# Fetching the last 128 rows of every group with SyncE and ScalarE row by row, in a three-layer graph network on one core

## The chip, the cores and the metric

One Trainium2 chip, one of its cores. The metric is the device time of one execution in microseconds (us). The kernel before was run three times.

## The reference

A layer norm of 6250 nodes of 256 features goes through three layers of a relational graph network with 200,000 edges of 8 types, and a feed-forward step whose log-sum form is a product of magnitudes and a product of signs.

```python
N, E, D, R, L = (6250, 31250, 256, 8, 3)      # 200000 edges are passed in
for l in range(n_layers):
    xr = jnp.einsum('nd,rde->rne', x, W_rel[l])
    msg = xr[edge_type, src]
    agg = jax.ops.segment_sum(msg, dst, num_segments=x.shape[0])
    x = jax.nn.relu(agg + x @ W_root[l] + bias[l])
...
x = x + _L0_gnn_ref(_layernorm(x, axis=-1), edge_index, edge_type_8, W_rel, W_root, bias)
x = x + _L0_ffn_ref(_layernorm(x, axis=-1)[None], weight, ffn_bias)[0]
```

In `_L0_ffn_ref`, out = sign(sign(x) @ sign(w).T) * (|x| @ |w|.T) + bias, scaled by the largest magnitudes of rows.

## The kernel before, in words

The edges are sorted by destination. A **triple** is 3 chunks of 128 edges, a **group** is 9 triples; there are 58 groups, and 49 tiles of 128 nodes. The node features of a layer lie in HBM (`node_table`, two of them, read and written in turn). Each layer goes through the 58 groups in order. In a group:

- GpSimd (`POOL`, L433) gathers the source rows of each chunk with one indirect DMA: 128 rows of 1 KB into `rows`, which holds one group's 27 chunks. The gather for a triple waits until TensorE has multiplied the triple nine before (`seg_ready`), and signals `gathered[k]`.
- TensorE (L454, `products`) multiplies the rows of triple k by a one-hot matrix, 12 matmuls of 128x128 in fp32. VectorE adds the result to `agg` (L1057, `agg_added`), and makes the next group's one-hots (L966).
- Behind the second triple of the next group TensorE multiplies `agg` by the relation weights, 32 matmuls (L523, `transform`). VectorE adds the result to the node sums `acc` (L1079, L1080), and ScalarE clears that half of `agg` (L755); the halves are used in turn by even and odd groups.
- Where a group is the first of a tile's, the tile before it has ended, and the group carries that tile's last steps (below: a *late* group). In layers 0 and 1 ScalarE makes `new_x` (L813) and stores it (L816), TensorE turns it behind triple 4, ScalarE copies it (`nextT`, L770), TensorE multiplies it behind triple 7, ScalarE copies the sum into `acc` (L762). In the last layer VectorE makes the layer norm and the magnitudes in the gaps behind triples 0 to 2; ScalarE gives the square root (L774), the sign (`sgn`, L784), the copies of what TensorE turned (`magT`, `sgnT`, L790, L791), the sign of the product (`osgn`, L797) and the output's store (L804). Each of these waits for another engine's step.
- In layer 0 SyncE also loads an `x_tile` per group, which TensorE turns behind triple 4 of its group, and ScalarE copies it to `xT` (L745).

In every **odd** group the last chunk isn't gathered by GpSimd: SyncE reads 128 byte offsets (`far_at`, L287, a load of 32 registers at a time) and issues 128 DMAs of one row each into `far_rows` (L354), once the even group before the last one fetched is multiplied (`multiplied`, L359). So GpSimd issues 27 gathers in an even group, 26 in an odd one, and 24 in the last group, whose last triple is empty.

```python
def fetch(layer, i, q):
    for p, start in zip(range(q * LOADS, (q + 1) * LOADS), far_starts(i, q)):
        sp.dma_start(far_row(p), far_from(layer, start)).then_inc(far_by_sp[layer][p // HALF], 16)
```

The order of each engine's work is written out by hand, and each engine issues its own in order. GpSimd's is unrolled; SyncE, ScalarE and TensorE have loops: SyncE one of 24 and one of 4 turns in layer 0 and one of 28 turns in each later layer, two groups a turn. A new layer's gathers start when the layer before has stored its last tile.

## Time and profile before

| | |
|---|---|
| median of 3 runs | 5928.23 us (5927.94 to 5928.28) |
| the profiled execution | 5926.47 us, its span 5924.7 us |
| GpSimd busy | 4371.6 us, 74% |
| TensorE busy (matmuls) | 4305.1 us, 73% |
| VectorE busy | 1828.7 us, 31% |
| ScalarE busy | 619.3 us, 10% |
| granted TensorE clock, mean | 0.894 |

The span runs from the first to the last instruction of the profiled execution. Busy time leaves out what issues DMAs, and register, branch and semaphore instructions, so SyncE has no busy time, and its work is read from its DMA queue's rows (`SPq`; `ACTq` is ScalarE's). An engine that is busy for 74% can still set the pace, if it can't issue faster.

### The profile page before, as it was taken

Reading aid. Unit: us, or ns where it says so; the run is one execution under the profiler, and the core shown is the slowest. Engines: PE = TensorE matmul, PEld = TensorE weight load, DVE = VectorE, ACT = ScalarE, POOL = GpSimd, SP = SyncE. Lnnn points to the kernel's source line nnn. Section 1 sums busy time; section 2 is a strip of 40 time slices with the busy share of each in tenths; the row PEclk is TensorE's granted clock in tenths of the full one; section 3 lists DMA queues with packets and bytes.
Section 4 is the critical chain, followed back from the end, with each engine's and each line's share of the span. In section 5 each row is a group of like instructions: output and inputs, shape, how many; then the busy total and the mean of one; then the engine's idle time right before and its main releaser. Section 6 shows DMA issues by size and latency. Waiting matters only on the chain.

```text
span 5924.7 us, 107591 instructions
## 1 busy us (share of the span) xinstructions
PE 4305.1 (73%) x26040; PEld 3885.7 (66%) x26041; DVE 1828.7 (31%) x3534; ACT 619.3 (10%) x848; POOL 4371.6 (74%) x4631
## 2 busy tenths in 40 slices
PE   3777777787787677777777777767777777677776
PEld 3666666676676666666666666656766667666666
DVE  4222222222222222222222222223334334333333
ACT  3101010101010000010001000001111011101111
POOL 5777777777777677777777777767777777777775
PEclk7989999989989899998999999989888888888898
DMA  6433343433443333333333333333333333333332
GB/s 196 116 113 115 114 115 114 115 114 114 114 116 114 104 111 111 110 111 110 110 110 111 110 110 111 110 104 112 113 113 115 113 113 114 113 112 114 112 113 85
DMA packets 301812, 672.72 MB, mean 114 GB/s; under 512 B 89440, under 2 KB 154181, under 8 KB 301670
## 3 DMA queue, kind: packets, MB, share of 16 engines
q0 software_dynamic: 221040, 603.88, 35.6%
q1 hardware_dynamic: 51928, 41.07, 2.3%
q10 hardware_dynamic: 28702, 26.46, 1.3%
q14 instruction: 124, 1.02, 0.1%
q8 instruction: 18, 0.29, 0.0%
HBM read 645.38 MB, written 25.68 MB: 113 GB/s over the span
## 4 chain that ended last, share of the span: by engine, by line
POOL 38%; PE 29%; issue 18%; DMA 8%; DVEq 2%; ACT 2%; DVE 2%; ACTq 0%; SPq 0%; POOLq 0%
POOL rows L433 38%; PE bank L454 16%; PE bank L523 11%; DMA rows<-node_table,idx 7%; ACT agg L755 2%; DVE agg L1057 1%; PE bank L655 1%; DVEq L1040 1%; DVEq L1043 1%; DVEq L1147 1%; PE bank L581 0%; PE bank L662 0%; PE bank L653 0%; ACT x_in L708 0%; DVE onehot L966 0%
## 5 line engine op out<-in xcount | busy, mean ns | idle before, releaser
L433 POOL DMA_INDIRECT rows<-node_table,idx x4605 | 4364.3, 948 | 1504.1 <-issue 1300.8
L454 PE MATMUL bank<-onehot,rows 128*128 128x128 f32 x18444 | 2683.6, 305 | 1431.6 <-DMA rows<-node_table,idx 665.1
L454 PEld LDWEIGHTS bank<-onehot,rows 128*128 128x128 f32 x18444 | 2520.7, 217 | 1597.7 <-issue 1578.5
L1057 DVE TENSOR_TENSOR agg<-bank,agg 128x256 f32 x1566 | 664.2, 424 | 2168.9 <-PE bank L454 1652.0
L523 PE MATMUL bank<-wrel,agg 128*128 128x256 f32 x5568 | 1266.3, 387 | 15.3 <-issue 14.0
L523 PEld LDWEIGHTS bank<-wrel,agg 128*128 128x128 f32 x5568 | 1071.3, 195 | 164.4 <-issue 21.6
L966 DVE TENSOR_TENSOR onehot<-bank,key 128x1152 f32<-128x1152 f32 x525 | 707.3, 1347 | 0.2
L755 ACT COPY agg<-zero_col 128x2304 f32 x174 | 367.3, 2111 | 2973.8 <-PE bank L523 2973.8
L1079 DVE SCALAR_TENSOR_TENSOR acc<-bank,in_first,acc 128x256 f32 x174 | 84.1, 484 | 1806.9 <-PE bank L523 1682.3
L762 ACT COPY acc<-bank 128x256 f32 (+1 forms) x98 | 36.5, 372 | 1071.4 <-PE bank L655 1071.4
L655 PE MATMUL bank<-wroot,nextT 128*128 128x256 f32 x392 | 146.3, 509 | 0.0
L655 PEld LDWEIGHTS bank<-wroot,nextT 128*128 128x128 f32 x392 | 85.0, 240 | 54.9 <-issue 45.1
L643 PE MATMUL bank<-ident_bf,sgn 128*128 128x128 bf16 x98 | 14.1, 228 | 108.2 <-issue 101.8
L653 PE MATMUL bank<-bias_bc,one_row 1*128 1x256 f32 x196 | 89.8, 547 | 1.5 <-ACT nextT L770 1.5
L643 PEld LDWEIGHTS bank<-ident_bf,sgn 128*128 128x128 bf16 x98 | 6.3, 97 | 117.4 <-issue 117.4
L1080 DVE SCALAR_TENSOR_TENSOR acc<-bank,in_second,acc 128x256 f32 x174 | 82.6, 475 | 0.0
L581 PE MATMUL bank<-wroot,xT 128*128 128x256 f32 x232 | 76.6, 464 | 0.0
L770 ACT COPY nextT<-bank 128x256 f32<-128x256 f32 x98 | 36.5, 372 | 374.9 <-PE bank L636 374.9
L1070 DVE TENSOR_TENSOR agg<-agg 128x256 f32<-128x256 f32 (+1 forms) x174 | 73.1, 420 | 0.0
L454 PE MATMUL bank<-onehot,far_rows 128*128 128x128 f32 x348 | 72.3, 292 | 0.0
L581 PEld LDWEIGHTS bank<-wroot,xT 128*128 128x128 f32 x232 | 55.5, 243 | 10.4
L454 PEld LDWEIGHTS bank<-onehot,far_rows 128*128 128x128 f32 x348 | 57.9, 209 | 0.0
(140 smaller groups left out, 844.7 us busy)
## 6 DMA issues: line engine op xcount, KB each, us to landing
far_rows<-node_table SPq DMA_DIRECT2D x10752, 1.0 KB
rows<-node_table,idx POOLq DMA_INDIRECT x4605
node_table<-new_x ACTq DMA_DIRECT2D x98, 128.0 KB
x_tile<-node_table SPq DMA_DIRECT2D x58, 128.0 KB
x_in<-in_x_dram SPq DMA_DIRECT2D x8, 768.0 KB, 11.2
wrel<-in_L_gnn_W_rel_dram SPq DMA_DIRECT2D x6, 1024.0 KB, 6.9
xres<-in_x_dram ACTq DMA_DIRECT2D x48, 128.0 KB
out_dram<-res ACTq DMA_DIRECT2D x48, 128.0 KB
```

Source lines behind the costliest of these rows:

```text
L433: pool.indirect_dma_start(rows[:, s:s + D], None, tables[layer % 2], bass.IndirectOffsetOnAxis(ap=idx[:, g * TPG + k, j:j + 1], axis=0),). ...
L454: last = nc.tensor.matmul(to[:, h, :], row, hot[:, hot_k * CH + j, :], start=(j == 0), stop=(j == CH - 1))
L523: last = nc.tensor.matmul(out_ps, agg[:, half * KH + h, r, 0:P], wrel[:, h, r * D:(r + 1) * D], start=(r == 0 and h == 0), stop=(r == R - ...
L581: last = nc.tensor.matmul(root_ps, xT[:, h, :], wroot[:, 0, h, :], start=(h == 0), stop=(h == KH - 1))
L653: nc.tensor.matmul(next_ps, one_row[:, :], bias_bc[0:1, layer + 1, :], start=True, stop=False)
L655: last = nc.tensor.matmul(next_ps, nextT[:, h, :], wroot[:, layer + 1, h, :], start=False, stop=(h == KH - 1))
L755: nc.scalar.copy(agg[:, ds(g % 2 * KH, KH), :, :].rearrange("p h r s -> p (h r s)"), zero_col[:, :].to_broadcast([P, KH * R * SLOTS])).the ...
L966: return nc.vector.tensor_tensor(onehot[:, b, :, :], place_ps.unsqueeze(1).to_broadcast([P, BATCH * CH, P]), key[:, ds(g * TPG + b * BATCH ...
L1057: nc.vector.tensor_tensor(window, seg[k % 3].rearrange("p h (r w) -> p h r w", r=R), window, ALU.add).then_inc(agg_added, 1)
L1070: nc.vector.tensor_tensor(agg[:, half, :, 0:WIN], agg[:, half, :, 0:WIN], agg[:, half, :, P:SLOTS], ALU.add).then_inc(agg_ready, 1)
L1079: nc.vector.scalar_tensor_tensor(sums_of(first), out_ps, in_first[:, ds(g, 1)], sums_of(first), ALU.mult, ALU.add)
L1080: nc.vector.scalar_tensor_tensor(sums_of(first + 1), out_ps, in_second[:, ds(g, 1)], sums_of(first + 1), ALU.mult, ALU.add).then_inc(group ...
```

## The change

- All groups but the last (57 of 58) have their last 128 rows fetched row by row: `far_rows` has two halves, for even and odd groups. GpSimd issues 26 gathers in each of them: 4518 in all instead of 4605.
- SyncE fetches 74 of the 128 rows of each group, ScalarE's queue 54. Both read the same `far_at`.
- SyncE fetches a group when the group two before it has been multiplied. Its loops are unrolled by four groups: 14 turns each, 12 and 2 in layer 0.
- ScalarE fetches the rows of the group behind its own while it works on a group. In layers 0 and 1 it issues 22 rows (`fetch_third`), then copies `next_ps` into `acc`, then 32 rows (`fetch_fourth`). In the last layer's late groups it issues 10 rows ahead of `magT`, 12 ahead of `osgn`, 10 ahead of the output's store and 22 behind it. Each batch stands twice in the program, once for each half of `far_rows`, with a branch.
- At the start of a layer both fetch group 0, ScalarE ahead of its first group.
- TensorE waits ahead of triple 8 for the two gathered chunks, two semaphores of SyncE and one of ScalarE.

```diff
-FETCHED = GROUPS // 2 - 1
-HALF = P // 2
+FETCHED = GROUPS - 1
 LOADS = 32
 QUARTERS = P // LOADS
+SP_ROWS = 74
+ACT_ROWS = P - SP_ROWS
+SP_HALF = SP_ROWS // 2
+ACT_TURNED, ACT_SIGNED = 20, 10
+SP_UNROLL = 4
...
+        far_rows = sb("far_rows", [P, 2 * D], fp32)
...
+            def multiplied(layer, g):
+                if not isinstance(g, int):
+                    sp.wait_ge(agg_added, g * TPG + (layer * TRIPLES + 3 - TPG))
+                    sp.sem_inc(sp_mark, 1)
+            def fetch(layer, g, b, q):
+                first, end = q * LOADS, min(SP_ROWS, (q + 1) * LOADS)
+                for p, start in zip(range(first, end), far_starts(SP, g, q, 0, end - first)):
+                    sp.dma_start(far_row(p, b), far_from(layer, start)).then_inc(far_by_sp[layer][b][p // SP_HALF], 16)
+            def first_layer(g, b, tile):
+                multiplied(0, g)
+                fetch(0, g, b, 0)
+                fetch(0, g, b, 1)
+                load_tile(g, tile)
+                fetch(0, g, b, 2)
             load_tile(0, 0)
             sp.wait_ge(far_at_ready, 1)
-            def first_layer(i, odd, even):
-                multiplied(0, i)
-                for q in range(QUARTERS // 2):
-                    fetch(0, i, q)
-                load_tile(i * 2 + 1, odd)
-                for q in range(QUARTERS // 2, QUARTERS):
-                    fetch(0, i, q)
-                load_tile(i * 2 + 2, even)
-            with sp.Fori(0, (TILES - 1) // 2) as i:
-                first_layer(i, i * 2 + 1, i * 2 + 2)
-            with sp.Fori((TILES - 1) // 2, FETCHED) as i:
-                first_layer(i, TILES - 1, TILES - 1)
+            for q in range(QUARTERS - 1):
+                fetch(0, 0, 0, q)
+            with sp.Fori(0, (TILES - 1) // SP_UNROLL) as i:
+                for m in range(1, SP_UNROLL + 1):
+                    first_layer(i * SP_UNROLL + m, m % 2, i * SP_UNROLL + m)
+            with sp.Fori((TILES - 1) // SP_UNROLL, FETCHED // SP_UNROLL) as i:
+                for m in range(1, SP_UNROLL + 1):
+                    first_layer(i * SP_UNROLL + m, m % 2, TILES - 1)
             load_tile(GROUPS - 1, TILES - 1)
             for layer in range(1, L):
                 sp.wait_ge(out_ready, layer * GROUPS)
                 load_weights(layer)
                 sp.wait_ge(stored, 16 * TILES * layer + 16)
-                with sp.Fori(0, FETCHED) as i:
-                    multiplied(layer, i)
-                    for q in range(QUARTERS):
-                        fetch(layer, i, q)
+                for q in range(QUARTERS - 1):
+                    fetch(layer, 0, 0, q)
+                with sp.Fori(0, FETCHED // SP_UNROLL) as i:
+                    for m in range(1, SP_UNROLL + 1):
+                        g = i * SP_UNROLL + m
+                        multiplied(layer, g)
+                        for q in range(QUARTERS - 1):
...
-                        for j in range(CH - 1 if g % 2 and k == TPG - 1 else CH):
+                        for j in range(CH - 1 if k == TPG - 1 else CH):
...
+            def far_landed(layer, g, b):
+                pe.wait_ge(gathered[TPG - 1], g * (16 * (CH - 1)) + (layer * FETCHED + 1) * (16 * (CH - 1)))
+                for h in range(2):
+                    pe.wait_ge(far_by_sp[layer][b][h], g * (8 * SP_HALF) + (2 - b) * 8 * SP_HALF)
+                pe.wait_ge(far_by_act[layer][b], g * (8 * ACT_ROWS) + (2 - b) * 8 * ACT_ROWS)
...
+            act.wait_ge(far_at_ready, 1)
+            def fetch_part(layer, g, b, q, first, end=LOADS):
+                for m, start in enumerate(far_starts(SCALAR, g, q, first, end)):
+                    act.dma_start(far_row(q * LOADS + first + m, b), far_from(layer, start)).then_inc(far_by_act[layer][b], 16)
+            def multiplied(layer, g):
+                if not isinstance(g, int):
+                    act.wait_ge(agg_added, g * TPG + (layer * TRIPLES + 3 - TPG))
+                    act.sem_inc(act_mark, 1)
+            def fetch_third(layer, g, b):
+                multiplied(layer, g)
+                fetch_part(layer, g, b, QUARTERS - 2, SP_ROWS % LOADS)
+            def fetch_fourth(layer, g, b):
+                fetch_part(layer, g, b, QUARTERS - 1, 0)
+            def fetch_by_turn(layer, g, b):
+                multiplied(layer, g)
+                fetch_part(layer, g, b, QUARTERS - 2, SP_ROWS % LOADS, ACT_TURNED)
+            def fetch_by_product(layer, g, b):
+                fetch_part(layer, g, b, QUARTERS - 2, ACT_TURNED)
+            def fetch_by_sign(layer, g, b):
+                fetch_part(layer, g, b, QUARTERS - 1, 0, ACT_SIGNED)
+            def fetch_by_store(layer, g, b):
+                fetch_part(layer, g, b, QUARTERS - 1, ACT_SIGNED)
+            def fetch_ahead(layer, g, part):
+                with act.If(g < FETCHED - 1):
+                    ahead = nc.s_assert_within(g + 1, 1, FETCHED - 1, skip_runtime_bounds_check_because="the branch is taken in front of the last fetched group")
+                    with act.If(g % 2 > 0):
+                        part(layer, ahead, 0)
+                    with act.Else():
+                        part(layer, ahead, 1)
+                    act.sem_inc(act_mark, 1)
             def group(layer, g, late=None):
                 gg = g + layer * GROUPS
                 if late:
@@ -743,13 +799,28 @@
                     act.wait_ge(xT_ps_ready, gg + 2)
                     act.sem_inc(act_mark, 1)
                     nc.scalar.copy(xT[:, :, :], xT_ps).then_inc(xT_ready, 1)
-                if late:
+                if layer < L - 1:
+                    fetch_ahead(layer, g, fetch_third)
+                    if late:
+                        with act.If(g < late[0]):
+                            next_sums(layer, late[1])
+                    fetch_ahead(layer, g, fetch_fourth)
+                elif late:
                     with act.If(g < late[0]):
-                        if layer < L - 1:
-                            next_sums(layer, late[1])
-                        else:
-                            turned_tile(late[1])
-                            out_of_tile(late[1])
+                        fetch_ahead(layer, g, fetch_by_turn)
+                        turned_tile(late[1])
+                        fetch_ahead(layer, g, fetch_by_product)
+                        sign_of_tile(late[1])
+                        fetch_ahead(layer, g, fetch_by_sign)
+                        out_of_tile(late[1])
+                        fetch_ahead(layer, g, fetch_by_store)
+                    with act.Else():
+                        fetch_ahead(layer, g, fetch_third)
+                        fetch_ahead(layer, g, fetch_fourth)
+                        act.sem_inc(act_mark, 1)
+                else:
+                    fetch_ahead(layer, g, fetch_third)
+                    fetch_ahead(layer, g, fetch_fourth)
                 act.wait_ge(out_ready, gg + 1)
                 act.sem_inc(act_mark, 1)
                 nc.scalar.copy(agg[:, ds(g % 2 * KH, KH), :, :].rearrange("p h r s -> p (h r s)"),
@@ -790,11 +861,14 @@
                 nc.scalar.copy(magT[:, :, :], mag_ps).then_inc(magT_ready, 1)
                 nc.scalar.copy(sgnT[:, :, :], sgn_ps).then_inc(sgnT_ready, 1)
-            def out_of_tile(t, last=False):
...
+                if layer:
+                    act.wait_ge(stored, 16 * TILES * layer + 16)
+                fetch_third(layer, 0, 0)
+                fetch_fourth(layer, 0, 0)
```

SyncE's first loop in layer 0, first of the kernel before: the loads of 32 offsets, the rows, and `x_tile` in the middle (L348, L350). These are the rows behind the loop's head at L372.

```order
L372 ISA
L287 ISA
L287 TENSOR_LOAD far_at
L354 DMA far_rows<-node_table 1x1024 x32
L287 ISA
L287 TENSOR_LOAD far_at
L354 DMA far_rows<-node_table 1x1024 x32
L348 ISA
L350 ISA
L350 DMA x_tile<-node_table 128x256
```

The same place now. The piece from the loop's head to the batch of 10 is one group, and it stands four times in the loop.

```order
L379 ISA
L292 ISA
L292 TENSOR_LOAD far_at
L366 DMA far_rows<-node_table 1x1024 x32
L292 ISA
L292 TENSOR_LOAD far_at
L366 DMA far_rows<-node_table 1x1024 x32
L353 REGISTER_ALU
L355 ISA
L355 DMA x_tile<-node_table 128x256
L292 ISA
L292 TENSOR_LOAD far_at
```

What moved: a turn of the loop was two groups with 128 rows and two `x_tile`; it is now four groups with 296 rows and four `x_tile`.

ScalarE in the last layer, inside the loop over tiles, from the copy of the turned magnitudes to the output's store. Before:

```order
L790 COPY magT<-bank 128x256
L791 COPY sgnT<-bank 128x256
L797 ACTIVATE osgn<-bank 128x256
L798 REGISTER_ALU
L804 ISA
L804 DMA out_dram<-res 128x256
```

Now, from `osgn` on (the batch of 12 rows stands ahead of it in the same form):

```order
L868 ACTIVATE osgn<-bank 128x256
L785 COMPARE_AND_BRANCH
L787 REGISTER_ALU
L787 COMPARE_AND_BRANCH
L292 ISA
L292 TENSOR_LOAD far_at
L756 DMA far_rows<-node_table 1x1024 x10
L787 UNCONDITIONAL_BRANCH
```

What moved: between two steps that stood next to each other there are now two branches, a register load and ten row DMAs; the second branch chooses between two copies of the batch. The loop over tiles has 216 row DMAs in the program, of which a group issues 54; the loops of the first two layers have 108.

## Rows read from the trace of the kernel before

**Rows 1.** GpSimd's gathers by their line: ns min/median/max, first and last start in us

```profile
L433 POOL DMA_INDIRECT rows<-node_table,idx x4605: 942/946/1241, 50.9 to 5882.9; - x192
```

**Rows 2.** Timeline, GpSimd, early, and where the last layer starts

```profile
92.27 0.95 POOL L433 DMA_INDIRECT rows<-node_table,idx  x1 [7.27 <-PE bank L454]
...
3956.96 0.94 POOL L433 DMA_INDIRECT rows<-node_table,idx  x1 [29.91 <-DMA node_table<-new_x]
3958.21 0.95 POOL L433 DMA_INDIRECT rows<-node_table,idx  x1 [0.30 <-issue]
```

**Rows 3.** Waits of TensorE, second layer, 2015 to 3965: us, times, longest

```profile
PE bank L454 <- DMA rows<-node_table,idx: 321.3, 207, 3.3
```

**Rows 4.** Waits of TensorE, last layer, 3965 to 5884

```profile
PE bank L454 <- DMA rows<-node_table,idx: 92.4, 61, 2.7
```

**Rows 5.** Timeline, ScalarE's clears of agg around three late groups

```profile
4674.05 2.11 ACT L755 COPY agg<-zero_col 128x2304 f32 x1 [30.06 <-PE bank L523]
...
4773.21 2.11 ACT L755 COPY agg<-zero_col 128x2304 f32 x1 [12.92 <-PE bank L523]
```

**Rows 6.** Waits of TensorE in those three groups, 4674.0 to 4773.2

```profile
PE bank L454 <- DVE agg L1057: 18.5, 6, 4.7
```

**Rows 7.** The chain that ended last, 4674 to 4708

```profile
by line: PE bank L454 42.2%; PE bank L523 21.1%; issue 16.4%; DVEq L1147 2.9%; DVE agg L1057 2.6%; PE bank L662 2.5%; DVEq L1040 2.5%; DVEq L1043 2.4%; PE bank L645 1.2%; DVEq L1057 0.8%; PE bank L643 0.8%; DVEq L1150 0.8%; PE bank L664 0.6
```

**Rows 8.** Waits of TensorE in the group before, 4641.9 to 4674.0

```profile
PE bank L454 <- DMA rows<-node_table,idx: 5.2, 3, 2.2
```

**Rows 9.** By source line: row DMAs, load of 32 registers, load of 2

```profile
L354 SPq DMA_DIRECT2D far_rows<-node_table x10752: 224/225/314, 87.0 to 5810.6; - x200
...
L287 SPq TENSOR_LOAD <-far_at x336: 2024/2036/2457, 84.8 to 5798.4; - x168
...
L827 ACTq TENSOR_LOAD <-end_row x144: 485/725/976, 154.7 to 5872.7; - x144
```

**Rows 10.** SyncE's queue in its first loop: timeline, and its wait

```profile
1024.16 22.99 SPq L354 DMA_DIRECT2D far_rows<-node_table  x64
1047.49 0.36 SPq L350 DMA_DIRECT2D x_tile<-node_table  x1
1060.73 0.27 SPq L354 DMA_DIRECT2D far_rows<-node_table  x1
...
SPq L359 <- DVE agg L1057: 10.1, 1, 10.1
```

**Rows 11.** The same place in its second loop

```profile
1711.81 0.37 SPq L350 DMA_DIRECT2D x_tile<-node_table  x1
1724.22 0.98 SPq L354 DMA_DIRECT2D far_rows<-node_table  x3
...
SPq L359 <- DVE agg L1057: 6.1, 1, 6.1
```

**Rows 12.** Timeline, ScalarE in a late group of layer 0

```profile
1011.29 0.38 ACT L745 COPY xT<-bank 128x256 f32<-128x256 f32 x1
1022.16 0.37 ACT L762 COPY acc<-bank 128x256 f32 x1 [10.49 <-PE bank L655]
1038.68 2.11 ACT L755 COPY agg<-zero_col 128x2304 f32 x1 [16.16 <-PE bank L523]
```

**Rows 13.** Timeline, ScalarE in a late group of the last layer

```profile
4681.37 0.29 ACT L774 ACTIVATE moments<-moments,eps_col 128x1 f32<-128x1 f32 x1 [5.21 <-DVE moments L1099]
...
4682.66 0.42 ACT L784 ACTIVATE sgn<-z 128x256 bf16<-128x256 f32 x1 [1.00 <-DVE z L1107]
4687.93 0.37 ACT L790 COPY magT<-bank 128x256 f32<-128x256 f32 x1 [4.85 <-PE bank L645]
...
4694.48 0.38 ACT L797 ACTIVATE osgn<-bank 128x256 f32<-128x256 f32 x1 [5.91 <-PE bank L664]
4699.72 0.36 ACTq L804 DMA_DIRECT2D out_dram<-res  x1
4707.79 2.11 ACT L755 COPY agg<-zero_col 128x2304 f32 x1 [12.92 <-PE bank L523]
```

More of the change, by code:

```diff
@@ L278, in gnn_ffn, with far_row, far_starts @@
         REST = FULL_TRIPLES - FULL_BLOCKS * P
-        def far_row(p):
-            return far_rows[p:p + 1, :].bitcast(u8)
+        def far_row(p, b):
+            return far_rows[p:p + 1, b * D:(b + 1) * D].bitcast(u8)
         def far_from(layer, at_byte):
             return table_bytes[layer % 2][:, ds(at_byte, ROW_BYTES)]
-        def far_starts(i, q):
+        def far_starts(engine, g, q, first, end):
             _, starts = nc.values_load_multi_w_load_instructions(
-                far_at[q:q + 1, ds(i * LOADS, LOADS)], engines=[SP], min_val=0, max_val=(N - 1) * ROW_BYTES,
+                far_at[q:q + 1, ds(g * LOADS + first, end - first)], engines=[engine], min_val=0, max_val=(N - 1) * ROW_BYTES,
                 skip_runtime_bounds_check_because="sources are nodes")
@@ L350, in load_tile @@
                 sp.dma_start(x_tile[:, :], tables[0][ds(tile * P, P), :]).then_inc(x_tile_loaded, 16)
-            def fetch(layer, i, q):
-                for p, start in zip(range(q * LOADS, (q + 1) * LOADS), far_starts(i, q)):
-                    sp.dma_start(far_row(p), far_from(layer, start)).then_inc(far_by_sp[layer][p // HALF], 16)
-            def multiplied(layer, i):
-                sp.wait_ge(agg_added, i * (2 * TPG) + (layer * TRIPLES + 3))
-                sp.sem_inc(sp_mark, 1)
+            def multiplied(layer, g):
+                if not isinstance(g, int):
+                    sp.wait_ge(agg_added, g * TPG + (layer * TRIPLES + 3 - TPG))
+                    sp.sem_inc(sp_mark, 1)
@@ L451, in products, with rows_of @@
                         row = of[:, s:s + P]
-                        if far and j == CH - 1:
-                            row = far_rows[:, h * P:(h + 1) * P]
+                        if far is not None and j == CH - 1:
+                            row = far_rows[:, far * D + h * P:far * D + (h + 1) * P]
                         last = nc.tensor.matmul(to[:, h, :], row, hot[:, hot_k * CH + j, :], start=(j == 0), stop=(j == CH - 1))
                 return last
-            def rows_of(layer, g, k, fetched=False):
+            def far_landed(layer, g, b):
[3 more added lines that the diff above has]
+                pe.wait_ge(far_by_act[layer][b], g * (8 * ACT_ROWS) + (2 - b) * 8 * ACT_ROWS)
+            def rows_of(layer, g, k, b=None):
                 if k < TPG - 1:
                     pe.wait_ge(gathered[k], (g + layer * GROUPS) * (16 * CH) + 16 * CH)
-                    return
-                before = layer * 16 * ((GROUPS - 1) * CH - FETCHED)
-                if not fetched:
-                    pe.wait_ge(gathered[k], g * (16 * CH - 8) + (before + 16 * CH))
-                    return
-                with pe.If(g < GROUPS - 1):
-                    pe.wait_ge(gathered[k], g * (16 * CH - 8) + (before + 16 * CH - 8))
-                    for h in range(2):
-                        pe.wait_ge(far_by_sp[layer][h], g * (8 * HALF) + 8 * HALF)
-                    pe.sem_inc(pe_mark, 1)
+                elif b == 0:
+                    far_landed(layer, g, 0)
+                else:
+                    with pe.If(g < FETCHED):
+                        far_landed(layer, g, 1)
+                        pe.sem_inc(pe_mark, 1)
             def extra_products(layer, g, more):
@@ L1004, in extra_tiles @@
                     dve.sem_inc(dve_mark, 1)
-                    with dve.If(g % 2 > 0):
-                        nc.vector.tensor_copy(rows[:, (TPG * CH - 1) * D:], far_rows[:, :]).then_inc(far_spread, 1)
-                    with dve.Else():
-                        dve.sem_inc(far_spread, 1)
+                    nc.vector.tensor_copy(rows[:, (TPG * CH - 1) * D:], far_rows[:, ds(g % 2 * D, D)]).then_inc(far_spread, 1)
                     dve.wait_ge(far_spread, groups + 1)
```

30 lines of the change are left out of this document (18 added, 12 removed).

## The prediction

> **What bounds the kernel now.** I began with GpSimd's gathers, since the page gives GpSimd the largest busy time but not whether it is ever held up. The view of their line [rows 1] shows 4605 gathers of 0.946 us between 50.9 and 5882.9 us. The timeline [rows 2] shows one every 1.25 us: 0.95 busy and a fixed 0.30 before the next, put down to issue and not to any semaphore. A group of 27 gathers takes 33.8 us and one of 26 takes 32.5, so two take 66.3. 4605 x 1.25 = 5756 us of the 5924.7. The rest is the start (50.9), the one real stall (7.3, row at 92.27), two layer boundaries (29.9 each, [rows 2]), the tail behind the last gather (41.8), and some 6 us that the last layer loses in small pieces: its 1535 gathers run from 3957.0 to 5882.9, 1.2555 us apart. At every group but the first, GpSimd sets the pace.
>
> Next I asked how much slower TensorE could be before it took over. In the second layer it waits 321.3 us for gathered rows [rows 3], 5.5 us in each of 58 groups, so its own group is under 33.1 - 5.5 = 27.6 us. Two layers of three are GpSimd's alone. The last layer differs: only 92.4 us of such waits [rows 4]. There most groups also end a node tile ("late" groups: the group's first triples carry the tile's output steps). ScalarE's clears of agg, one to a group [rows 5], give three late groups in a row in 4773.21 - 4674.05 = 99.16 us, 33.05 us each. TensorE waits in them for VectorE (18.5 us, the first of its rows) and for no gather at all [rows 6], and the chain over one of them holds TensorE, VectorE and issue and no GpSimd [rows 7]. The group that isn't late, ahead of them, waits 5.2 us for gathers in its 32.1 [rows 8]: 27 us of its own. 49 tiles end in 58 groups, the last behind the loop: 48 of the layer's 57 periods are late, 9 aren't, so the last layer without GpSimd would be 48 x 33.05 + 9 x 27 = 1829 us, against 57 x 33.1 = 1889 with it. Both matter there.
>
> **What the change takes away.** 29 even groups a layer lose one gather: 87 x 1.25 = 108.8 us of GpSimd's time. Each group is then 26 gathers, 32.5 us (32.6 in the last layer by its 1.2555). In the first two layers TensorE's 27.6 lies far below. The whole 72.5 us comes off there, if the rows arrive.
>
> **SyncE's part.** The price of a row is in [rows 9, 10]: 64 rows and one register load in 22.99 us; less the load's 2.04 that is 0.327 us a row (0.225 of it the DMA instruction). A load of 2 registers takes 0.725 [rows 9], one of 32 takes 2.04: 0.044 a register, so 10 registers 1.1, 12 1.2, 22 1.6. Per group now: 74 x 0.327 + 2.04 + 2.04 + 1.1 = 29.4 us; in the first layer x_tile is issued too (0.7), 30.1. The trace of before doesn't show a loop of 296 rows, but it shows what a jump back can cost. In the first loop, from the end of the x_tile issue (1047.85) to the next row (1060.73) are 12.88 us, of which 10.1 is the wait and 2.04 the load, 0.7 the rest [rows 10]. In the second loop, with the same 128 rows, 1712.18 to 1724.22 is 12.04, of which 6.1 and 2.04 are explained and 3.9 are left [rows 11]. So a jump back costs 3.2 us more there. A loop of 128 rows is evidently at the edge of what an engine keeps; 296 rows lie beyond it. I take 3.2 us per 4 groups, 0.8 each: 30.2 us (30.9 in the first layer) against 32.5. SyncE keeps pace, with 1.6 us over in its worst layer, and the second buffer lets it be a group ahead.
>
> The Trainium skill, Runtime: NRT & Kernel Launch, section Instruction fetch mechanics, says that most engines hold two 16 KiB blocks of instructions and that a taken branch to a place outside them waits for a fetch; the stall in the second loop agrees, and by the page both SyncE's new loops and ScalarE's last one must stall. The same section puts a register load at about 200 ns a register. By that SyncE's 74 registers would take 14.8 us, a group 39 us, and SyncE would be the bound; the row has 2.04 us for 32, 0.064 each; the measurement decides, and the rule gets no chance.
>
> **ScalarE's part, first two layers.** 54 rows a group in batches of 22 and 32. Each batch also has its branches and a wait, for which I take the 0.7 us that the loop's end cost SyncE [rows 10], an upper bound. 22 rows: 7.2 + 1.6 + 0.7 = 9.5 us from the xT copy (1011.29): done at 1021, ahead of the acc copy at 1022.16. 32 rows: 10.5 + 2.0 + 0.7 = 13.2: done at 1035.8, and the clear comes at 1038.68 (1037.5 at the new pace) [rows 12]. Behind a late clear stands new_x, for which TensorE's turn waits, but there are some 2 us over, and the loop holds 108 rows, fewer than the loop that ran without the stall. Cost 0.
>
> **ScalarE's part, last layer.** Four batches between the output's steps [rows 13]. 10 rows cost 3.3 + 1.1 + 0.7 = 5.1 against 5.3 from sgn (4682.66) to magT. 12 rows: 3.9 + 1.2 + 0.7 = 5.8 against 6.5 to osgn. 10 rows: 5.1 against 5.2 to the output's store. 22 rows: 9.5 against 7.7 from the store's end (4700.08) to the clear (4707.79): 1.8 late. The clear isn't urgent itself, since the half that it clears is used a group later; what is late next is the square root, and it stood idle 5.21 us before it [rows 13]. That leaves 3.4 us. But this loop holds 216 rows, and by [rows 11] its jump back costs 3.2. 0.2 us are left, and less where the period is shorter: of the three, the first has 33.7 us [rows 5, 13], the other two 32.7 on average. The first three batches fill their gaps within some 0.2 us. I let a late group grow by 0.45 us, to 33.5; with no jump it would be 33.1. 48 x 33.5 + 9 x 27 = 1851 us, still below GpSimd's 57 x 32.6 = 1858. The late groups come in runs of about five; nine triples of gathered rows are 32 us of buffer against a lag of 5 x 0.9. The layer follows GpSimd; for the ends of runs, and for TensorE being further behind at the tail, I take 5 us.
>
> **Start.** SyncE now fetches group 0 as well, 30 us from about 85, and x_tile of group 1 comes behind another 64 rows, near 141. TensorE then stands at group 1, but GpSimd resumed at 92.27 [rows 2] and needs group 1's sixth triple freed only at 143.6. I take 1 us, bounds 0 and 6. The other layers' first groups have 32.5 us for a fetch of 30.
>
> **Sum.** Against the profiled execution's 5926.5 us: - 108.8 + 5 + 1 = 5823.7. The median of the runs lies 1.8 us higher: 5825.5, say 5826, 1.7% faster.
>
> **Rivals.** *ScalarE bounds the late groups mildly.* If its row is 5% dearer than SyncE's, or the branches cost 1 us a batch, a late group is near 35 us: 48 x 35 + 9 x 28 = 1932, 74 above GpSimd's, about 5900. For it: three gaps without room. Against: it goes by SyncE's bound for the branches already. With half of that, 5860. Chance 0.2 for 5845 to 5905.
> *Slower: ScalarE stalls twice in a late group*, at the jump over the other branch (108 rows long) and at the jump back. Each costs 3.2 [rows 11]: 36.7 a late group, 30 another, 48 x 36.7 + 9 x 30 = 2032, 174 over: 5998. It decides the sign from about 36.2 us a late group. Against it: a jump forward may land in what is fetched already. Chance 0.06.
> *Slower: the two queues hinder each other.* SyncE's row at 0.357 instead of 0.327 would make its group 33.1 in the first layer, and the gain there is gone; 20% dearer makes 35 us in all 171 groups, 6200 and more. The row instruction never took over 0.314 us with 0.225 the median [rows 9], beside gathers and stores. Chance 0.04.
> *Nothing gained*, because TensorE holds every layer, is excluded by 321.3 us of waits in the second. *The gathers' own pace changes* by under 0.3%: 15 us either way, inside the range.
>
> **Chances and range.** Forecast, 5814 to 5845: 0.68. Mild rival 0.2. Slower than before 0.09; near no change 0.03. What a measurement of this kernel tells from no change is about 0.2%, 12 us. Faster 0.88. The range takes the forecast and most of the mild rival: 5814 to 5880.
>
> **What would show it.** 4518 gathers at 1.25 us; clears 32.5 us apart in the first two layers; TensorE waits for gathers there of some 4.9 us a group, and none for far_rows behind group 0; SyncE's wait for agg short, 2 to 3 us a group; in the last layer late groups of 33.1 to 33.6 and the idle time before the square root gone or nearly. I am wrong if far_rows releases TensorE in steady state, or if ScalarE's square root comes over 8 us behind the clear and GpSimd starts to wait for seg_ready.

## The result, and the profile after

| | before | after |
|---|---|---|
| median | 5928.08 us (4 runs, 5927.15 to 5928.28) | 6206.81 us (4 runs, 6205.4 to 6212.09) |
| span of the profiled execution | 5924.7 us | 6206.2 us |
| GpSimd's gathers | 4605 | 4518 |
| a late group of the last layer (ScalarE's clear to clear), mean of 48 | 33.4 us | 40.6 us |
| one of the last layer's 9 other periods, mean | 32.4 us | 33.1 us |

The ratio is 1.0472, 95% interval 1.0454 to 1.049: slower by 279 us, where 102 us of gain were forecast. The miss is 381 us.

GpSimd's view comes first again: its line, and where the layers meet.

```profile
L446 POOL DMA_INDIRECT rows<-node_table,idx x4518: 940/946/1439, 50.8 to 6147.7; - x197
  issue: 1299.1, 4250
  PE bank L467: 467.3, 265
...
3860.57 0.95 POOL L446 DMA_INDIRECT rows<-node_table,idx  x1 [0.30 <-issue]
3886.15 0.94 POOL L446 DMA_INDIRECT rows<-node_table,idx  x1 [24.64 <-DMA node_table<-new_x]
```

The last layer's gathers start at 3886.15, where they started at 3956.96 before [rows 2]: 70.8 us gained in two layers, where 72.5 were forecast. Everything is lost behind that, in one layer: its gathers run for 2262 us and not for 1926. The waits from 4050 to 6150 (engine, line, what it waits for: us in total, times, longest) show who is late there.

```profile
ACT agg L826 <- issue: 1227.5, 53, 31.8
PEld bank L658 <- issue: 465.6, 45, 16.6
PE bank L658 <- DVE mag L1194: 457.8, 45, 16.4
POOL rows L446 <- PE bank L467: 401.4, 97, 10.2
...
DVE moments L1181 <- ACT moments L845: 365.7, 45, 13.8
```

Read it from below. VectorE waits for ScalarE's square root (45 times, one for nearly each late group), TensorE for the magnitudes that VectorE makes of it, GpSimd for TensorE. ScalarE's clear waits for nobody: "issue" says that nothing in the profile holds it. ScalarE is the bound, and the chain over the same stretch, by line, lies on it:

```profile
by line: ACTq L756 35.6%; issue 28.8%; ACTq L292 21.6%; ACTq L905 2.2%; PE bank L467 2.2%; ACTq L878 1.0%; ACTq L787 1.0%; DVE z L1184 0.9%; ACT sgnT L862 0.7%; ACT moments L845 0.7%; PE bank L538 0.5%; DVE moments L1181 0.4%; DVE onehot L1
```

L756 are ScalarE's row DMAs, L292 its register loads, and 28.8% are "issue". One late group, ScalarE alone, by the timeline:

```profile
5008.19 2.11 ACT L826 COPY agg<-zero_col 128x2304 f32 x1 [21.63 <-issue]
5013.45 0.29 ACT L845 ACTIVATE moments<-moments,eps_col 128x1 f32<-128x1 f32 x1 [3.15 <-issue]
5013.77 0.36 ACTq L850 DMA_DIRECT2D xres<-in_x_dram  x1
5014.76 0.42 ACT L855 ACTIVATE sgn<-z 128x256 bf16<-128x256 f32 x1 [1.00 <-DVE z L1184]
5017.69 3.38 ACTq L756 DMA_DIRECT2D far_rows<-node_table  x10
5021.25 0.37 ACT L861 COPY magT<-bank 128x256 f32<-128x256 f32 x1 [6.08 <-DVE agg L1134]
...
5023.06 4.01 ACTq L756 DMA_DIRECT2D far_rows<-node_table  x12
5027.26 0.38 ACT L868 ACTIVATE osgn<-bank 128x256 f32<-128x256 f32 x1 [5.36 <-PE bank L679]
5028.95 3.33 ACTq L756 DMA_DIRECT2D far_rows<-node_table  x10
5032.67 0.40 ACTq L878 DMA_DIRECT2D out_dram<-res  x1
5038.78 7.45 ACTq L756 DMA_DIRECT2D far_rows<-node_table  x22
5049.24 2.11 ACT L826 COPY agg<-zero_col 128x2304 f32 x1 [21.60 <-issue]
```

`magT` and `osgn` have another engine as their releaser, but ScalarE issues rows until 5021.07 and 5027.07, 0.2 us ahead of either, so it hardly waits there. The rows cost nearly what [rows 9] gave: 22 in 7.45 us, where 7.2 were forecast. The rest lies in the gaps between these lines, and the chain names what fills them:

```profile
5008.68 3.05 issue
...
5015.40 2.19 ACTq L292
...
5021.99 0.98 ACTq L292
...
5027.68 1.18 ACTq L292
...
5033.77 4.92 ACTq L292
...
5046.36 2.58 issue
```

Two stalls, 3.05 at the jump back to the loop's start and 2.58 at the jump over the copies of the batches for groups that aren't late (108 rows long; from L785 to L824, in all 48 late groups, whichever half of `far_rows` they filled). And two register loads far dearer than the forecast had them: 22 registers 4.92 us instead of 1.6, the first 10 2.19 instead of 1.1. But 12 registers took 0.98 and the other 10 1.18, as forecast. Price and count don't go together. What the dear ones share is that they start at register 10 of their quarter of `far_at`; the cheap ones start at 0 and 20.

### The profile page after: what moved, and what is told of

Read it like the earlier page. It is cut to its first block, busy times and chain, and to the rows that moved or that the text cites. A ratio compares the mean times of both kernels' runs of the same rounds, so it can differ in the third digit from the quotient of the medians.

```text
span 6206.2 us, 133833 instructions
## 1 busy us (share of the span) xinstructions
PE 4280.1 (69%) x26040; PEld 3891.4 (63%) x26041; DVE 1830.1 (29%) x3534; ACT 619.4 (10%) x848; POOL 4286.6 (69%) x4544
## 4 chain that ended last, share of the span: by engine, by line
ACTq 23%; issue 22%; POOL 19%; PE 14%; SPq 12%; DMA 5%; DVE 2%; DVEq 2%; ACT 1%
POOL rows L446 19%; ACTq L756 13%; SPq L366 9%; ACTq L292 8%; PE bank L538 7%; PE bank L467 7%; DMA rows<-node_table,idx 4%; SPq L292 3%; ACTq L905 1%; DVEq L1120 1%; DVEq L1117 1%; DVE agg L1134 1%; ACTq L878 0%; ACT agg L826 0%; ACTq L787 0%
## 5 line engine op out<-in xcount | busy, mean ns | idle before, releaser
L446 POOL DMA_INDIRECT rows<-node_table,idx x4518 | 4279.3, 947 | 1853.8 <-issue 1299.1
L467 PE MATMUL bank<-onehot,rows 128*128 128x128 f32 x18096 | 2648.0, 306 | 1183.3 <-DVE agg L1134 574.6
L467 PE MATMUL bank<-onehot,far_rows 128*128 128x128 f32 x696 | 140.5, 285 | 0.0
L670 PE MATMUL bank<-wroot,nextT 128*128 128x256 f32 x392 | 125.9, 449 | 0.0
L651 PE MATMUL bank<-ident,new_x 128*128 128x128 f32 x196 | 43.4, 307 | 114.6 <-ACT new_x L887 114.6
L467 PEld LDWEIGHTS bank<-onehot,far_rows 128*128 128x128 f32 x696 | 111.9, 202 | 0.0
L651 PEld LDWEIGHTS bank<-ident,new_x 128*128 128x128 f32 x196 | 25.2, 155 | 120.4 <-issue 120.4
L668 PE MATMUL bank<-bias_bc,one_row 1*128 1x256 f32 x196 | 76.5, 473 | 1.3 <-ACT nextT L841 1.3
```

Of the source, the lines that this page charges most:

```text
L446: pool.indirect_dma_start(rows[:, s:s + D], None, tables[layer % 2], bass.IndirectOffsetOnAxis(ap=idx[:, g * TPG + k, j:j + 1], axis=0),). ...
L467: last = nc.tensor.matmul(to[:, h, :], row, hot[:, hot_k * CH + j, :], start=(j == 0), stop=(j == CH - 1))
L670: last = nc.tensor.matmul(next_ps, nextT[:, h, :], wroot[:, layer + 1, h, :], start=False, stop=(h == KH - 1))
```

## The experiments

### What makes a late group 41 us

**e1_aligned** starts each of ScalarE's loads at the multiple of four below its first register and throws the first ones away (10 becomes 8).

```diff
+            skip = first % 4
-                far_at[q:q + 1, ds(g * LOADS + first, end - first)], engines=[engine]
+                far_at[q:q + 1, ds(g * LOADS + first - skip, end - first + skip)], engines=[engine]
-            return starts
+            return starts[skip:]
```

> Edit: a register load that would begin at offset 10 of a line of 32 begins at 8, with two registers more that nobody uses; same rows, same order. Theory A (ScalarE bounds the last layer's late groups at 41 us, and 4.3 us of them are two loads of registers that begin off a 16-byte boundary, 4.95 us for 22 registers and 2.2 for 10): loads of 24 in 1.75 us and of 12 in 1.0, late groups near 36.7, total 5985, between 5965 and 6005. Rival B (only the two stalls behind jumps, 2.7 and 2.8 us, are in excess): 6207, within 12. Rival C (54 row DMAs on ScalarE are too much for the late groups whatever the loads and jumps cost, the gaps between the output's steps being overfull): the chain takes the saved time up elsewhere, 6100 or more.

Measured: 6026.23 us (6021.71 to 6035.64), ratio to before 1.0168 (1.0151 to 1.0185). 181 us come back with no other edit. A late group took 37.4 us. The loads are a cause (rival B had 6207, rival C 6100 or more), but their price was set somewhat too high: 6026 lies 21 us above the expected range.

**e2_shared** leaves the loads as they are and shortens the last layer's loop: late and other groups share the four batches, and only the output's steps stand under the condition of a late group. The loop is 339 instructions long instead of 578, and the jump over the second copy is gone.

```diff
-                elif late:
-                    with act.If(g < late[0]):
-                        fetch_ahead(layer, g, fetch_by_turn)
...
+                elif late:
+                    for part, step in ((fetch_by_turn, turned_tile), (fetch_by_product, sign_of_tile), (fetch_by_sign, out_of_tile)):
+                        fetch_ahead(layer, g, part)
+                        with act.If(g < late[0]):
+                            step(late[1])
+                    fetch_ahead(layer, g, fetch_by_store)
```

> Edit: in the last layer late and other groups share the four batches, the output's steps alone stand under a branch, so the loop over tiles holds 108 row DMAs and not 216, and the jump over the other branch is gone; loads as in the changed kernel. Theory B (5.5 us of a late group are stalls behind the two jumps): late groups 35.5, total 5943; if only the forward jump's stall goes, 38.3 and 6077. Theory A alone (loads): 6207, within 12. Rival C: 6100 or more with both stalls gone.

Measured: 5941.88 us (5935.86 to 5948.43), ratio 1.003 (1.002 to 1.0039), where theory B had 5943. A late group takes 35.4 us, both stalls are gone, and the instruction queue (q14 on the page) moved 414 packets, where the changed kernel moved 744.

**e3_both** has both edits.

> Both edits. A and B together are additive as long as ScalarE is the bound: 41.0 - 4.3 - 5.5 = 31.2 us, under GpSimd's 32.6, so the layer follows GpSimd and the total is 5826 to 5835; with the backward stall left, late groups of 34 and 5850. Rival C: above 5928, since the rows alone are too many.

Measured: 5825.32 us (5820.18 to 5829.05), ratio 0.983 (0.9814 to 0.9847), on the chip where before took 5923.66. It beats both kernels, 1 us under the expected 5826 to 5835. A late group with the loads short and the stalls gone, from the timeline, and the waits from 4050 to 5700:

```profile
4664.40 2.11 ACT L820 COPY agg<-zero_col 128x2304 f32 x1 [15.39 <-issue]
4669.08 0.29 ACT L839 ACTIVATE moments<-moments,eps_col 128x1 f32<-128x1 f32 x1 [2.57 <-DVE moments L1170]
...
4687.76 0.39 ACTq L872 DMA_DIRECT2D out_dram<-res  x1
4690.39 7.49 ACTq L757 DMA_DIRECT2D far_rows<-node_table  x22
4698.43 2.11 ACT L820 COPY agg<-zero_col 128x2304 f32 x1 [15.83 <-issue]
```

```profile
POOL rows L447 <- issue: 384.5, 1260, 0.3
...
ACT moments L839 <- DVE moments L1170: 110.2, 42, 5.2
...
POOL rows L447 <- PE bank L468: 16.5, 54, 0.3
```

The square root waits for VectorE again, as it did before [rows 13], and GpSimd waits for TensorE 16.5 us in all, where it waited 401.4 in the changed kernel. ScalarE is no longer the bound.

**e4_hybrid** is the changed kernel in layers 0 and 1, and the kernel before in the last.

> Edit: layers 0 and 1 as changed, the last layer as before (GpSimd gathers the even groups' last rows, SyncE the odd groups', ScalarE none). If all of the loss is ScalarE's in the last layer and the first two layers gained what the gathers saved (70 us at the last layer's start), the total is the last layer's start as changed, 3887, plus the last layer as before, 1968: 5857, within 8. If the changed kernel's first layers hand on a debt (TensorE or the queues further behind), more than 5865.

Measured: 5857.81 us (5856.33 to 5858.76), ratio 0.9886 (0.987 to 0.9903), 65.9 us faster than before, where 5857 was expected. The gain of two layers is real, whatever the third does.

The four kernels with all steps in place form a square:

| loads \ stalls | both stalls | none |
|---|---|---|
| start at register 10 | 6206.8 (after) | 5941.9 (e2) |
| start at 8 | 6026.2 (e1) | 5825.3 (e3) |

(After was timed beside a before of 5928, the others beside one of 5924.) Over 48 late groups the loads alone cost (5941.9 - 5825.3)/48 = 2.4 us a group, the stalls alone 4.2, both 7.9. By the durations the loads are 4.4 us longer (4.92 - 1.6 and 2.19 - 1.1) and the stalls 5.5 (2.67 and 2.79 on average): sum 9.9. So some 1.3 to 2.0 us of either hide in ScalarE's slack, once; the second cause pays almost in full. That is why the parts add up to less (6.6) than the whole.

These prices charge everything to the late groups, and the 9 other periods of the layer grew as well. From clear to clear, on average:

| | e3 | e2 (loads) | e1 (stalls) | after (both) |
|---|---|---|---|---|
| 48 late groups | 33.5 | 35.4 | 37.4 | 40.6 |
| 9 others | 28.2 | 31.3 | 30.5 | 33.1 |

### The price of a register load

**e10_live** puts twelve loads behind e3's last tile, from one row of `far_at`, with DMAs that use the registers.

```diff
+            for count, first in ((22, 10), (22, 8), (22, 9), (22, 0), (22, 6), (22, 4), (10, 10), (10, 8), (10, 0), (10, 2), (10, 20), (12, 20)):
+                _, starts = nc.values_load_multi_w_load_instructions(
+                    far_at[3:4, ds(first, count)], engines=[SCALAR], ...)
+                for start in starts:
+                    act.dma_start(scratch[rows_read:rows_read + 1, :], far_from(L - 1, start)).then_inc(x_res_loaded, 16)
```

> The kernel of e3_both, and behind its last output tile twelve register loads on ScalarE, each followed by DMAs that use the registers (22 or 10 rows each into a scratch tensor), so that the loads stay in the program. Kernel e3_both plus about 75 us. Theory L1: a load whose first register's number isn't a multiple of four (the first byte not on 16 bytes) costs some 0.2 us a register, every other one 0.06 to 0.12: 22 registers from 10, 9 and 6 take 4.4 to 5.0 us, 22 from 8, 0 and 4 take 1.4 to 1.7; 10 from 10 and 2 take 2.0 to 2.2, 10 from 8, 0 and 20 take 0.8 to 1.2, 12 from 20 takes 1.0. Rival L2: it is the count that matters (24 and 32 were fast, 22 slow): 22 registers cost 4.4 us or more from any place. Rival L3: it is the boundary that lies inside (32 bytes): 22 from 4 and 10 from 20 are slow as well.

Measured, by the source line in narrow windows, in the order 22 registers from 9, 0, 6, 4 and 10 registers from 10, 8, 2 (ns, and the start in us):

```profile
L926 ACTq TENSOR_LOAD <-far_at x1: 4708/4708/4708, 8474.3 to 8474.3; - x1
L926 ACTq TENSOR_LOAD <-far_at x1: 1694/1694/1694, 8493.1 to 8493.1; - x1
L926 ACTq TENSOR_LOAD <-far_at x1: 4707/4707/4707, 8509.1 to 8509.1; - x1
L926 ACTq TENSOR_LOAD <-far_at x1: 1708/1708/1708, 8527.9 to 8527.9; - x1
L926 ACTq TENSOR_LOAD <-far_at x1: 2176/2176/2176, 8543.7 to 8543.7; - x1
L926 ACTq TENSOR_LOAD <-far_at x1: 1002/1002/1002, 8552.5 to 8552.5; - x1
L926 ACTq TENSOR_LOAD <-far_at x1: 2172/2172/2172, 8567.3 to 8567.3; - x1
```

> Edit: e3_both with loads of registers at ScalarE's end, 22 registers from offsets 0, 2, 4, 6, 8, 9, 10 and 10 registers from offsets 0, 2, 4, 8, 10, 12, 16, 20, each from two partitions; only their own durations are of use. Theory A (the price is set by whether a load starts on a multiple of 4 registers, 16 bytes): 22 registers 1.5 to 1.9 us from 0, 4, 8 and 4.7 to 5.0 from 2, 6, 9, 10; 10 registers 0.8 to 1.2 from 0, 4, 8, 12, 16, 20 and 2.2 from 2 and 10. Rival D (it is the crossing of a line of 16 or 32 registers by the load, or its end, that costs): 22 from 4 dear as well, since it crosses 16.

### Where the stall at the jump comes from

**e5_pad32** is e3_both with 32 semaphore increments ahead of ScalarE's first loop, **e7_after_pad125** the changed kernel with 125.

```diff
+            for _ in range(32):
+                act.sem_inc(act_mark, 1)
             act.wait_ge(ends_loaded, 16)
```

> Edit: e3_both with 32 semaphore increments more in ScalarE's program while it is idle at the start (2 us, hidden), which shifts all that follows by 32 instructions. Theory P (the stall behind a jump back hangs on where the loop lies against blocks of instructions that the engine holds, as SyncE's two loops of 128 rows had it before): with the blocks' borders where SyncE's loops put them, the last layer's loop now lies in three blocks, 2.8 us behind each jump back in it and none in the first layers; ScalarE's group grows from 31 to 34 us, total 5840 to 5855. Rival (only the loop's length counts): no stall anywhere, 5825 within 10.

> Edit: the changed kernel itself with 125 increments; its loads of 22 registers from offset 10 stay at 4.7 us. Theory P with the loads: the first layer's ScalarE loop, which filled 32.0 us of a group, grows to 34.8 and becomes the bound there: 57 x 2.3 = 130 us more than the changed kernel, 6330, within 30; the last layer about as before. Rival (length only): 6207 within 15.

In e5 the jump back of the last layer's loop took 3.16 us (median of 47), in e3 0.29. The kernels without the increments took 0.29 on e5's own chip too (e8), and the two pairs on the last two chips repeat it: 3.21 against 0.29 (e12, e11) and 3.18 against 0.29 (e16, e17). So the same loop of 339 instructions stalls or not by where it lies. In e7 the jump back of layer 0's loop never took over 1.39 us (0.26 median), while the last layer's loop stalled as in the changed kernel (2.5 back, 2.7 forward). Theory P got e5's loop right and e7's first loop wrong. That position matters is shown; which positions are bad isn't. Length counts too: the loop of 578 instructions stalled at both jumps in each kernel that has it (after, e1, e7, e15), the one of 339 at neither in e2 and e3.

### The same kernels where the kernel before is slower itself

All runs from e5 on were made on three other chips, on which the kernel before took 7547, 7694 and 7714 us. Nothing of these times can be set beside those above; each stands beside before on its own chip.

| kernel | median, us | before there | ratio (95%) |
|---|---|---|---|
| e5_pad32 | 8303.88 | 7547.44 | 1.1014 (1.0992 to 1.1036) |
| e7_after_pad125 | 8459.55 | 7547.44 | 1.122 (1.119 to 1.1251) |
| e8_loads (= e3_both) | 8304.54, 1 run | 7547.44 | 1.100 |
| e9_behind | 8676.0 | 7547.44 | 1.1505 (1.1467 to 1.1542) |
| e10_live | 8595.09, 1 run | 7694.26 | 1.117 |
| e11_both_again | 8415.2 | 7694.26 | 1.0937 (1.0903 to 1.097) |
| e12_pad32 | 8379.78 | 7694.26 | 1.0883 (1.0849 to 1.0918) |
| e13_behind | 8773.2 | 7694.26 | 1.1392 (1.1355 to 1.143) |
| e14_before | 7729.88, 1 run | 7713.64 | 1.002 |
| e15_after | 8514.21 | 7713.64 | 1.1046 (1.0987 to 1.1105) |
| e16_pad32 | 8408.92 | 7713.64 | 1.0908 (1.0878 to 1.0937) |
| e17_both | 8428.18 | 7713.64 | 1.0929 (1.0896 to 1.0962) |

> The kernel of e3_both again, as the partner of the other kernels of this job. On a chip where the kernel before takes about 5925 us: 5825, ratio 0.983. On a chip where the kernel before takes about 7550 us, by the run e8_loads: 8304, ratio 1.10. If e3_both's gain was luck of one job, the ratio is 1.00 or more on a chip of 5925 us as well.

> The kernel before, for its profile beside the others of this job. On a chip where it takes about 5925 us: the profile as shown before. On a chip where it takes about 7600 us, theory M (there the issuing of rows is dear: SyncE's 32 rows take 16 us and not 10.5, by e8_loads): its SyncE rows take 16 us per 32 as well, SyncE or the rows' landing is what TensorE waits for in the layers in which it fetches them, and the layers or groups without rows run at their usual pace. Rival N (the chip slows every engine's stream alike): groups with and without rows are slower by the same share, 28 per cent.

> The changed kernel. On a chip of 5925 us for the kernel before: 6207, ratio 1.047, and 380 us above e17_both. On a slow chip: 8400 to 8600, by the run e7_after_pad125 (8460).

> As e11_both_again: 5825 (ratio 0.983) on a chip of 5925 us for the kernel before; ratio 1.09 to 1.10 on a slow chip.

e3_both, 1.7% faster on the first chip, is 9 to 10% slower here, three times. The source view of SyncE's rows tells the difference; first e14_before, then e17_both, with [rows 9] as the partner of the first.

```profile
L354 SPq DMA_DIRECT2D far_rows<-node_table x10752: 1/224/1431, 89.8 to 7606.4; - x200
...
  PE bank L454: 57.8, 4
```

```profile
L367 SPq DMA_DIRECT2D far_rows<-node_table x12654: 1/224/1442, 85.6 to 8359.2; - x198
...
  PE bank L468: 1375.2, 107
```

The median row DMA is as short as before, but there are pauses that the first chip doesn't have. In e14 SyncE's stream pauses over 0.5 us 2642 times (115 times in the profile of before), mostly for 0.7 us (2329 times), at times for twice that; 32 rows take 17.1 us in the median and not 10.4. Before asks SyncE for 64 rows a group and has 41 us a group here (45 in the last layer); e17 asks for 74 and three loads, and its groups take 49.7, 45.7 and 47.5 us in the three layers. TensorE waits for SyncE's rows (last line: 1375.2 us, 107 times), which on the first chip it did in no group of steady state. TensorE's waits in e17:

```profile
PE bank L468 <- DMA far_rows<-node_table: 1173.8, 82, 27.1
PE bank L468 <- issue: 810.5, 464, 25.9
PE bank L525 <- DMA x_tile<-node_table: 688.6, 56, 14.9
```

Theory M (the issuing of rows is dear there) has its first part; its second, that before runs as usual where it fetches no rows, wasn't separated, and what makes the pauses wasn't found. TensorE's granted clock is lower too (0.784 on average in e14, 0.894 in the profile of before), which doesn't explain pauses on SyncE.

There is a second reason why the change can't gain here. GpSimd doesn't set the pace even in e14:

```profile
POOL rows L433 <- PE bank L454: 1428.3, 465, 9.2
```

In the profile of before these waits are 108.8 us in all. The gathers themselves are as short as ever (946 ns in the median, mostly 1.25 us apart), so GpSimd's stream isn't slowed as rival N has it for every engine; but a gather less saves nothing while GpSimd waits for TensorE.

With SyncE as the bound of e17, ScalarE's excess mostly hides. e15_after is 86 us above e17_both where it was 381 above e3_both, and the stall that 32 fillers bring back costs nothing (e12 35 us below e11, e16 19 below e17, e5 level with e8). So the price of the jump-back stall alone stays open; only the two stalls together have one (4.2 us a late group).

> The kernel of e3_both with 32 increments of a semaphore ahead of ScalarE's first loop, which shift its instructions; in an earlier run this brought back the stall at the jump back of the last layer's loop (3.1 us, 48 times). Theory F (a stall costs what is over ScalarE's slack of a late group: the slow loads, 4.4 us a group, cost e2_shared 2.3 a group over e3_both, so the slack is 2.1): 0.8 to 1.0 us in each of 48 groups, e3_both plus 40 to 50, about 5870. Rival G (ScalarE is the bound of the late groups with no slack): plus 140, about 5965. Rival H (the stall is hidden): within 10 us of e3_both.

> As e12_pad32. On a chip of 5925 us for the kernel before: theory F e17_both plus 40 to 50, rival G plus 140, rival H within 10 us. On a slow chip: within 30 us of e17_both, as in two jobs.

**e9_behind** and **e13_behind** are one kernel, e3_both with the output's steps first in a late group and both batches of rows behind them.

```diff
-                    for part, step in ((fetch_by_turn, turned_tile), (fetch_by_product, sign_of_tile), (fetch_by_sign, out_of_tile)):
...
+                    with act.If(g < late[0]):
+                        turned_tile(late[1])
+                        sign_of_tile(late[1])
+                        out_of_tile(late[1])
+                    fetch_ahead(layer, g, fetch_third)
+                    fetch_ahead(layer, g, fetch_fourth)
```

> Edit: e3_both, but the last layer's late groups issue all 54 rows behind the output's store, in two batches, and none between the steps. If the four batches use time that ScalarE has anyway between the output's steps, taking them away costs what they hid: the 18.8 us from the square root to the store, then 54 rows in about 22.7, then 2.3 to the next square root: 43.8 us a late group instead of 33.1, 48 x 10.7 = 510 more, 6340. If the placing doesn't matter: 5825.

> The kernel of e3_both, but in the groups behind which an output tile is due ScalarE takes the three steps first and then both batches of rows (22 and 32), not four batches between the steps. Theory J (the rows between the steps lie in waits for VectorE and TensorE that ScalarE has anyhow; behind them they are added): ScalarE's late group goes from 33 to about 41 us, times 48: e3_both plus 370 to 390, about 6200, slower than the kernel before. Rival K (the rows are a group ahead, so that their place doesn't matter): within 30 us of e3_both.

It is 371 us above e8 and 358 above e11: 7.7 and 7.5 us a late group, near theory J's 370 to 390, though this was stated for a faster chip; e9's own expectation of 510 was too high. No jump of ScalarE stalls in either, so the difference is the place of the batches. Batches between the steps lie in waits that ScalarE has anyhow. That part of the change does what it should.

## Why the prediction was wrong

- *"87 x 1.25 = 108.8 us"*: right in mechanism and size. 70.8 us came off in two layers, and e3, with the last layer mended, gained 98 of the 102 us. That e3's 5825.3 met the sum of 5826 is in part luck: before ran at 5923.7 on that chip, and the sum has a jump-back stall in every late group that e3 hasn't.
- *SyncE, "30.2 us against 32.5", "1.6 us over in its worst layer"*: right in its outcome, with less room than stated. Its rows took 0.32 to 0.33 us, its jump back 2.6 to 3.35 on average once in four groups, and `far_rows` held TensorE in steady state nowhere. But in layer 0 it never had time to spare: from jump back to jump back its loop took 31.9 us a group in eleven turns, where 30.9 were forecast, and between 200 and 2000 it waited for `agg` once. TensorE waited for `x_tile` there (33 times and 135.8 us in e3, never in before). On the other three chips this is the step that fails.

```profile
PE bank L524 <- DMA x_tile<-node_table: 36.6, 16, 7.0
...
SPq L361 <- DVE agg L1134: 1.1, 1, 1.1
```

- *ScalarE in the first two layers, "cost 0"*: nearly. It has 22 registers from 10 there as well (4.74 us), so it used 3.1 us more than forecast, and TensorE waited 107.9 us for `new_x` between 200 and 3860 (2.8 before, 6.0 in e3, where the loads are aligned); GpSimd's pace held.
- *"10 registers 1.1, 12 1.2, 22 1.6"*: **the first step that failed.** I took a price of 0.044 us a register from loads of 32, which all start on 16 bytes, and of 2, which start anywhere but are too short to tell (0.49 to 0.50 us from every start in the last layer of before), and applied it to loads of 22 and 10 from register 10. Measured 2.19 for the first 10 and 4.92 for the 22. The Trainium skill, Runtime: NRT & Kernel Launch, section Instruction fetch mechanics, says some 200 ns a register; I wrote that the row refuted it and gave it no chance. The row refuted it for loads like its own. An estimate from the page's figure gives 4.4 us for 22 registers, near the 4.7 to 4.9 measured, and 2.0 for 10 against 2.2. The trace disagrees with the page for aligned loads (0.06 to 0.12 a register) and agrees for the others.
- *"a jump forward may land in what is fetched already"*, chance 0.06: **the second.** Both stalls of a late group came, 2.67 and 2.79 us on average in 48 and 47 groups. The rival stood there with its place and price; it had been argued away by a guess, though the loop was twice as long as the one of [rows 11], which had stalled. It was priced at 36.7 us a late group; e1, which has the stalls without the loads, measured 37.4. The rival's "about 36.2", where the sign turns, doesn't follow from its own sum: 102 us over the forecast's 1863 for the layer are 35.3 to 35.7 us a late group, with the others at 30 to 28. e2, at 35.4, was 0.3% slower than before.
- *"0.2 us are left"*: the step that should have set the chances. A late group's sum had no room, and the branches, the loads and the jumps in it stood on no row of their own kind. The missed loads (4.4) and the missed forward stall (2.7) are the 7.1 us by which an average late group (40.6) exceeds its 33.5, and 7.1 x 48 = 341 of the 381. The other periods, 33.1 us and not 27, add 9 x 6.1 = 55, less the 12 by which the forecast's layer (1858 + 5) lay over its late and other groups (1851). The base was a little low too: three late groups gave 33.05, all 48 average 33.4.

The range reached to 5880 and left both out. The rival "ScalarE stalls twice" covered one of the two causes, and its chance was too small for a path without slack.

## What to carry to other kernels

When work is put into an engine's gaps, write down the room left in each period and how often it comes; with 0.2 us of it 48 times, a cost that no row of the trace shows at that size and alignment is the forecast, not a detail. Start bulk register loads on 16 bytes even if it means to load some for nothing. Keep alternatives in a loop short: share what both branches do and put the condition round the rest, for the copy costs its jump as well as its length.

## What the runs showed of the hardware

- On ScalarE a load of 22 registers from SBUF took 1.7 us from a 16-byte boundary (elements 0, 4, 8) and 4.7 from elements 6 and 9; 10 took 1.0 (0, 8, 20) and 2.2 (2, 10).
- The same loop of 339 instructions jumped back in 0.29 us, and in 3.16 to 3.21 with 32 instructions more ahead of it, on three chips. One of 578 stalled in all four kernels that have it, 2.5 to 2.8 us on average at its jump back and 2.6 to 2.7 at a jump forward.
- On three of the four chips that the experiments ran on the kernel before took 7547 to 7714 us instead of 5924, with pauses of about 0.7 us in SyncE's stream (in ScalarE's too where it issues rows: 1319 in e17, 38 in e3), and a change that moves work from gathers to 74 single-row DMAs a group on SyncE turned from 1.7% faster to 9 to 10% slower. Whether it is the chip or its state at that hour is open.
